# One more order of the pieces of a transformer layer: 392 places, the fillers and who starts the restacking DMAs

## The reference

```python
for i in range(NL):                                       # NL = 6
    xn = _adaln(x, noise_emb, n1_w[i], n1_b[i])
    q, k, v = jnp.split(xn @ qkv_w[i].T, 3, axis=-1)
    q, k = _rope(q.reshape(B, L, H, HD)), _rope(k.reshape(B, L, H, HD))
    ...
    x = x + _attn(q, k, v, src_mask).reshape(B, L, D) @ so_w[i].T
    xn = _adaln(x, noise_emb, n2_w[i], n2_b[i])
    q = _rope((xn @ cq_w[i].T).reshape(B, L, H, HD))
    k = _rope((context @ ck_w[i].T).reshape(B, LC, H, HD))
    ...
    x = x + _attn(q, k, v, ctx_mask).reshape(B, L, D) @ co_w[i].T
    xn = _adaln(x, noise_emb, n3_w[i], n3_b[i])
    x = x + (jax.nn.gelu(xn @ f1_w[i].T + f1_b[i], approximate=False) @ f2_w[i].T + f2_b[i])
```

## Time and profile before

| | us |
|---|---|
| runs of the kernel before | 3232.94, 3234.14, 3237.18 (median 3234.14) |
| profiled execution | 3232.67 |
| its span, first to last instruction | 3230.8 |
| PE busy in the span | 2923.1 (90%) |
| DVE busy | 2161.5 (67%) |
| ACT busy | 1896.3 (59%) |
| POOL busy | 820.1 (25%) |
| DVE, L816, the maxima of self attention | 961.1 |
| ACT, L686, the exponentials | 943.0 |
| PE, L533, values of self attention | 509.2 |
| PE, L360, fillers | 262.7 |

### The profile page before, as it was taken

The page is one execution under the profiler, slowest core; times in us unless marked ns, Lnnn a source line. Parts: engine busy times, 40 slices in busy tenths (PEclk is TensorE's granted clock), DMA queues, the critical chain, the costliest instruction groups (busy, mean ns, idle before and its releaser), DMA issues.

```text
span 3230.8 us, 44892 instructions
## 1 busy us (share of the span) xinstructions
PE 2923.1 (90%) x15691; PEld 1031.2 (32%) x15691; DVE 2161.5 (67%) x3813; ACT 1896.3 (59%) x2677; POOL 820.1 (25%) x1327
## 2 busy tenths in 40 slices
PE   7998999979999999999999857999999998999978
PEld 2474344322322223232232222232322223232226
DVE  4316887658496786958668377769596776858634
ACT  5533444437667585766758534858577585766742
POOL 0003555532212222232213102212222222231211
PEclk9999999989999999999999877999999999999989
DMA  1101000001111111111101001111111111111130
GB/s 46 59 1 27 1 1 1 12 22 41 39 28 39 36 40 37 45 33 37 42 25 49 28 8 42 31 31 49 40 35 34 44 31 37 50 34 32 40 128 7
DMA packets 125506, 110.10 MB, mean 34 GB/s; under 512 B 49978, under 2 KB 116068, under 8 KB 125284
## 3 DMA queue, kind: packets, MB, share of 16 engines
q1 hardware_dynamic: 108004, 91.51, 9.5%
q10 hardware_dynamic: 17280, 15.74, 1.6%
HBM read 41.96 MB, written 0.52 MB: 13 GB/s over the span
## 4 chain that ended last, share of the span: by engine, by line
PE 66%; DVE 14%; SPq 8%; ACT 5%; issue 3%; DMA 3%; POOL 1%; ACTq 0%; DVEq 0%; POOLq 0%
PE ps L533 11%; SPq L437 8%; PE ps L471 6%; DVE arena L816 5%; PE ps L504 4%; PE ps L360 4%; PE ps L602 3%; PE ps L645 3%; DMA arena<-arena 3%; PE ps L661 3%; PE ps L1531 3%; PE ps L479 3%; PE ps L1519 2%; PE ps L574 2%; PE ps L585 2%
## 5 line engine op out<-in xcount | busy, mean ns | idle before, releaser
L686 ACT ACTIVATE arena<-ps 128x1024 f32<-128x1024 f32 x960 | 943.0, 1022 | 184.6 <-PE ps L504 180.0
L816 DVE TENSOR_REDUCE arena<-ps 128x1 f32<-128x512 f32 x1536 | 961.1, 684 | 100.9 <-PE ps L471 92.3
L533 PE MATMUL ps<-arena 128*32 128x512 f32 x3840 | 509.2, 609 | 1.2
L471 PE MATMUL ps<-arena 49*128 49x512 bf16 x1536 | 382.2, 389 | 83.9 <-DMA arena<-arena 37.0
L504 PE MATMUL ps<-arena 52*128 52x512 bf16 x1920 | 348.8, 387 | 34.0 <-ACT arena L686 22.0
L818 DVE TENSOR_REDUCE arena<-ps 128x3 f32<-128x462 f32 (+1 forms) x576 | 305.3, 580 | 110.9 <-PE ps L479 106.3
L913 POOL TENSOR_TENSOR arena<-arena,zeros 128x16 bf16<-128x16 f32 x192 | 42.4, 221 | 1192.6 <-DVE arena L816 769.0
L360 PE MATMUL ps<-consts 128*128 128x512 f32 x508 | 262.7, 624 | 24.4 <-DVE arena L2123 23.7
L471 PEld LDWEIGHTS ps<-arena 49*128 49x128 bf16 x1536 | 101.9, 93 | 498.3 <-DVE arena L816 419.9
L923 POOL TENSOR_TENSOR arena<-arena 128x512 f32<-128x512 f32 x96 | 122.8, 1279 | 323.2 <-ACT arena L716 323.2
L1596 ACT ACTIVATE arena<-ps 128x1024 f32<-128x1024 f32 x96 | 98.3, 1023 | 156.1 <-DVE ps L1681 152.8
(11 more groups left out here) (385 smaller groups left out, 4272.3 us busy)
## 6 DMA issues: line engine op xcount, KB each, us to landing
arena<-arena SPq DMA_DIRECT2D x624, 64.0 KB
arena<-arena ACTq DMA_DIRECT2D x240, 64.0 KB
arena<-we_dram SPq DMA_DIRECT2D x24, 578.5 KB, 7.7
w<-weights_dram SPq DMA_DIRECT2D x26, 320.0 KB, 3.1
w<-weights_dram SPq DMA_DIRECT2D x13, 512.0 KB, 4.1
arena<-arena SPq DMA_DIRECT2D x384, 6.0 KB
arena<-arena SPq DMA_DIRECT2D x288, 19.2 KB
w<-weights_dram SPq DMA_DIRECT2D x39, 128.0 KB, 2.2
```

The source lines that it names most:

```text
L471: pe.matmul(s_bank(slot + r), qst[b][rows, idx, P * qt:P * (qt + 1)], kst[b][rows, idx, :], start=True, stop=True).then_inc(s_full, 1)
L533: mm = pe.matmul(bank(7)[32 * j:32 * j + 32, :], v, prob[:, slot, j, :], start=(g % 2 == 0 and kt == 0), stop=(a == 0 and g % 2 == 1 and k ...
L686: act.activation(prob[:, chunk_no(b, a, g, kt) % NPROB, 2 * p:2 * p + 2, :], e_bank(slot).rearrange("p (j n) -> p j n", j=2), ACT.Exp, sca ...
L816: op = ve.tensor_reduce(nmax[:, g % 2, r, n:n + 1], s_bank(slot + r), AX.X, ALU.max, negate=True)
```

## The change

It gives another list of places for the same 392 pieces, another set of fillers and another set of slots that ScalarE begins (8 and not 10 in a layer). The code that runs a piece is the same. Of the table, whose rows tell little by themselves, three lines stand here:

```diff
-    ('inv', 0): [[134, 160], [297, 304]],
+    ('inv', 0): [[117, 153], [293, 303]],
-    ('f2',): [327, 428],
-    ('gain',): [-77, 95, 227],
+    ('f2',): [330, 430],
+    ('gain',): [-78, 86, 304],
...
-        ACT_STACKS = (("st", 0, 0, 2), ("st", 0, 1, 0), ("st", 0, 2, 5), ("st", 1, 0, 0), ("st", 1, 0, 4),
-                      ("st", 1, 1, 1), ("st", 1, 1, 2), ("st", 1, 1, 5), ("st", 1, 2, 1), ("st", 1, 2, 3))
-        FILL = {('center', 0, 0): 1, ('center', 0, 2): 1, ('out', 0, 1): 1, ('out', 1, 1): 3, ('proj', 1, 2):
-                1, ('score', 0, 0, 0, 2): 1, ('score', 0, 0, 0, 5): 1, ('score', 0, 0, 0, 6): 1, ('score', 0,
-                0, 0, 7): 1, ('score', 0, 0, 1, 0): 1, ('score', 0, 0, 1, 4): 1, ('score', 1, 1, 0, 0): 2,
-                ('var', 0, 2): 1}
+        ACT_STACKS = (("st", 0, 0, 0), ("st", 0, 1, 4), ("st", 1, 0, 0), ("st", 1, 0, 1), ("st", 1, 0, 4),
+                      ("st", 1, 1, 5), ("st", 1, 2, 0), ("st", 1, 2, 1))
+        FILL = {('center', 0, 2): 1, ('out', 0, 1): 1, ('out', 1, 1): 3, ('score', 0, 0, 0, 1): 1, ('score',
+                0, 0, 0, 2): 1, ('score', 0, 0, 0, 3): 1, ('score', 0, 0, 0, 4): 1, ('score', 0, 0, 0, 7): 1,
+                ('score', 0, 0, 1, 0): 1, ('score', 0, 0, 1, 4): 1, ('score', 1, 0, 0, 0): 1, ('score', 1, 0,
+                2, 1): 1, ('score', 1, 1, 0, 0): 2, ('var', 0, 2): 1}
```

More of the change, by code:

```diff
@@ L131 @@
-    ('st', 1): [[63, 78, 83, 80, 64, 81], [91, 73, 70, 88, 87, 85], [308, 311, 317, 309, 310, 312]],
-    ('ktail',): 185,
-    ('vals',): [4, 119, -1],
-    ('f1',): [[320, 323], [424, 426]],
-    ('f2',): [327, 428],
-    ('gain',): [-77, 95, 227],
-    ('biasf',): 167,
-    ('load',): {'cout': 560, 'cross': 306, 'ffn': 584, 'n0': 46, 'n1': 284, 'n2': 392, 'self': 174, 'sout':
-        341},
+    ('score', 0, 0): [[0, 1, 2, 3, 4, 5, 7, 8], [9, 11, 15, 18, 19, 22, 24, 29], [33, 35, 37, 41, 43, 45, 48,
+        50], [56, 69, 72, 77, 82, 87, 89, 93]],
@@ new lines @@
+    ('score', 0, 1): [[228, 230, 233], [236, 239, 245], [250, 255, 259], [263, 265, 273]],
+    ('score', 1, 0): [[98, 101, 104, 108, 111, 115, 118, 122], [125, 128, 130, 134, 136, 139, 144, 146], [154,
+        155, 159, 161, 166, 168, 172, 174], [176, 183, 190, 197, 203, 205, 208, 211]],
+    ('score', 1, 1): [[317, 318, 320], [321, 323, 325], [333, 336, 338], [341, 343, 349]],
+    ('msplit', 0, 0): [12, 39, 57, 103],
+    ('msplit', 0, 1): [240, 251, 260, 275],
+    ('msplit', 1, 0): [124, 151, 184, 217],
@@ new lines @@
+    ('pv', 1, 0): [[160, 178, 179, 194], [201, 209, 213, 215], [231, 237, 241, 248], [252, 257, 264, 269]],
+    ('pv', 1, 1): [[346], [363], [372], [373]],
+    ('tail',): [[274, 290], [344, 370]],
+    ('pvt',): [[[282, 288], [298, 299]], [[364, 367], [374, 381]]],
+    ('evac', 0): [[92, 148], [289, 300]],
+    ('evac', 1): [[216, 270], [368, 382]],
+    ('sel', 0): [[97, 152], [292, 301]],
+    ('sel', 1): [[227, 272], [377, 384]],
+    ('inv', 0): [[117, 153], [293, 303]],
+    ('inv', 1): [[232, 276], [378, 385]],
@@ new lines @@
+    ('out',): [[164, 307], [285, 388]],
+    ('center',): [[-55, 170, 312], [44, 291, 402]],
+    ('var',): [[-50, 175, 313], [49, 295, 408]],
+    ('apply',): [[-44, 180, 315], [55, 296, 419]],
+    ('proj',): [[-39, -37, 185, 83], [58, 61, 302]],
+    ('hi',): [[-36, -31, 189, 113], [62, 66, 305]],
+    ('st', 0): [[-12, -16, -17, -26, -3, -30], [-21, -2, -13, -1, -6, -9], [200, 221, 224, 199, 219, 222], [119,
+        191, 186, 162, 169, 193]],
+    ('st', 1): [[65, 76, 94, 64, 75, 63], [67, 79, 84, 81, 80, 90], [309, 311, 316, 308, 310, 306]],
@@ L140 @@
+    ('ktail',): 218,
+    ('vals',): [6, 150, -5],
+    ('f1',): [[319, 322], [426, 428]],
+    ('f2',): [330, 430],
+    ('gain',): [-78, 86, 304],
+    ('biasf',): 243,
+    ('load',): {'cout': 539, 'cross': 335, 'ffn': 533, 'n0': -45, 'n1': 246, 'n2': 405, 'self': 196, 'sout':
+        324},
 }
```

60 lines of the change are left out of this document (17 added, 43 removed).

## The result

The changed kernel takes 3,215.55 us (median of six runs, 3,212.27 to 3,225.77), the kernel before on the same chip 3,233.92 us (3,225.64 to 3,238.47). The ratio is 0.995, 95% interval 0.9934 to 0.9966: about 18 us faster, where 17 were forecast. The span of the profiled execution is 3,210.2 us, before 3,230.8.

A forecast was written before the change was run, and what follows sets the result against it. PE was taken as the fullest engine, with DVE, PE or a chain of waits setting the pace by stretch. Terms summed to -1.4 us a layer, times 12 -16.8, from 3,232.7 to 3,215.9, plus 1.5: 3,217 us; range 3,202 to 3,243.

The forecast's parts named there:

- Join: Between layers: `vals 2` no longer stands between the first two scores, so DVE's gap goes; -0.3 us a layer (-0.6 to 0).
- Restacking for batch 1: Before batch 1's first score: SyncE begins 16 DMAs, not 14, mostly covered by DVE's shuffle; +0.3 us (0 to +1.4).
- Cross query of batch 0: Its restacking: SyncE's 12 DMAs, before 10, cost +1.3 us, cancelled by earlier rope work; 0 (-0.5 to +1.3).
- PE's work: Up to batch 1's norm: `gain 2` and a PV piece leave the full stretch, a filler enters; -0.4 us (-1.0 to +0.5).
- The denominators ahead of the variance: Batch 1's cross norm: earlier inverse keeps POOL's multiplication off DVE's TENSOR_SCALAR; -0.8 us a layer (-0.9 to +0.3).
- FFN of batch 0: `f2 0` starts about 1.2 us later, more scores precede the norm's matmuls, DVE gaps pay; -0.2 us (-0.9 to +1.2).
- Last restacking: End of the layer: 20 DMAs on SyncE as before; 0.
- the full engine: Rival, no change: PE waits at the next place for what it gains; 3,228 to 3,240, middle 3,234 us; chance 0.18.
- The clock: Rival, slower: with two fillers gone nearby, one more clock fall in each layer adds 30 us; 3,247 us; chance 0.11.
- SyncE's queue: Rival, slower: both additional slots paid whole, PE's work gives nothing, layer 1.4 us longer; 3,251 us; chance 0.11.
- three marks set for "wrong": Batch 1's first score waits over 1 us; clock 0.50 in most layers; norm behind `f2 0` later than 169.3 us.
- marks for "right": TENSOR_SCALAR 0.49 us; second-score gap under 0.2; 16 DMAs about 11.2; DVE idle under 0.4; layers near 188.8 us.

The follow-up runs named there:

- e5: The changed kernel with `vals 2` behind the first score of a layer again, its fillers unchanged: 3,237.59 us, ratio 1.0009 to the kernel before.
- e12: e9 with slot (1,1,2) of batch 1's restacking begun by ScalarE, so SyncE has 14 DMAs there, not 16: 3,202.97 us, ratio 0.99.
- e7: The changed kernel with `gain 2` back at its earlier place, in the stretch that PE fills: 3,226.91 us, ratio 0.9964.
- e11: e9 without the one filler that the change put ahead of a score of batch 1: 3,206.77 us, ratio 0.9894.
- e1: The changed kernel with `inv 0,1,0` behind the variance of batch 1's cross norm again: 3,217.86 us, ratio 0.995.
- e2: The kernel before with only `inv 0,1,0` moved ahead of the variance of batch 1's cross norm: 3,232.32 us, ratio 1.0002.
- e9: The changed kernel with the multiplication of `inv 0,1,1` done by VectorE behind its rope, not by POOL: 3,203.58 us, ratio 0.9895.
- e8: The changed kernel with the pieces around `f2 0` (places 319 to 342) in the order of the kernel before: 3,226.48 us, ratio 0.997.
- e6: The changed kernel with two fillers back, ahead of batch 1's cross query projection and batch 0's next norm: 3,225.19 us, ratio 0.9969.
- e3: The changed kernel with POOL's multiplication of `inv 0,1,1` waiting for the rope's sum L872 on DVE: 3,221.58 us, ratio 0.9946.
- e10: The kernel before, old order, with both multiplications `inv 0,1,*` on VectorE and not POOL: 3,231.52 us, ratio 0.9976.

## Why the prediction was right, step by step

The forecast was right: 3,217 for 3,215.55 us, faster. That it was right to 1.5 us is in good part luck: four terms were off in size or mechanism, and their errors went both ways (batch 1's restacking and the denominators came out some 0.8 and 0.6 us a layer worse than forecast, PE's work and the FFN 0.8 and 0.4 better). The forecast was -1.4 us a layer; measured are -1.5 over ten layers, -1.2 by the medians of clean layers and -0.8 in the pair of the table, whose rows the parts below follow:

- *Join*: -0.3 forecast, -0.47 measured at the second score. That it counts at all is shown by e5.
- *Restacking for batch 1*: +0.3 forecast. Measured, the join's gain and 0.68 more are gone at that score, +1.1. SyncE starts 0.7 us sooner in the layer (0.3 forecast) and ends 0.7 later, with 1.46 more of issuing; the shuffle was the cover named, but DVE still idles 0.64. It lies near the upper end of the range given (+1.4), and it is the largest miss in size. The sentence that SyncE is full for its 9.80 us was true, and the conclusion from it was half of the matter: the transfers need as long, within a microsecond, and 1.2 us less issuing gave 0 to 0.3 in e12. The Trainium skill (DMA: Bandwidth & Descriptors, "Issuing engines are not separate DMA queues") says that issuing from several engines saves only the sequencer's time, which is usually small beside the transfer. e12 agrees with the first half, which I had set aside; the second does not hold here, with 11.26 us of issuing beside some 11 us of transfers.
- *Cross query of batch 0* and *PE's work*: 0 and -0.4 forecast, from batch 1's first score to the norm -1.2 measured. `gain 2` is 0.6 of it (e7). The PV piece that went ahead of batch 1's first score can give up to 1.06, which no run tests. The filler that I had set against it costs nothing (e11), since DVE sets the pace where it stands: that was the error. (The change has one more filler there than the prediction counts, ahead of batch 1's very first score; PE still waits 0.70 us behind it.)
- *The denominators ahead of the variance*: -0.8 forecast. L853 became fast as said, -0.86 up to the norm's application, and 0.69 went back at L872, 3 us further on. This is the step that failed: the path. I had taken the chain to the restacking to run through the norm, and it ran through POOL's second multiplication, behind which L872 ends by 0.55 us in every layer. e1 and e2 measure the net as 0.15 to 0.17 us, e9 shows what lay behind it. The Trainium skill (SBUF — State Buffer, "Who interferes with whom") says that a VectorE instruction with two SBUF inputs and a GpSimd instruction that reads SBUF exclude each other, and that the later one waits for the whole of the earlier. The trace agrees: DVE's sum started 0.06 us behind POOL's multiplication, took 1.75 - 0.69 = 1.06 us more than alone, and ended 0.55 us behind it. I had quoted it and not looked for the next meeting, although L872 took 1.07 us and not 0.69 already in the kernel before.
- *FFN of batch 0*: -0.2 forecast, -0.60 measured. Undoing its order (e8) gives back 0.33 up to the norm, counted from the layer's start. The filler that the change took out ahead of that norm is the other part: with it back (e6) the way from `f2 0` to the norm is 7.54 us and not 6.67. The two are more than the 0.60 together; I have not separated them further.
- *Last restacking*: 0 forecast. The layer of the table loses 0.5 us there. But from the end of SyncE's last issue to the first score on PE it takes 1.72 to 2.39 us in the layers of before and 1.91 to 2.40 after, in no order, so this looks like scatter.

Of the rivals, the full engine would have given 3,234: PE's place as the bound held, but in the waits beside it there was something to gain. The clock's place was named rightly; its count went from four to five in the ten layers. SyncE's queue was half right, as said. Of the three marks set for "wrong" two did not come: the first score of batch 1 waits 0.70 us and not over 1, and the norm behind `f2 0` is applied at 167.55 us (168.0 by the prediction's start of a layer), not behind 169.3, but for the layers with low clock. The third, a clock of 0.50 somewhere in most layers, did come as it stands: in eight of all twelve. It was a poor mark, since the kernel before has it in seven. Of the marks for "right" the idle DVE (0.64 for 0.4) failed.

A sum and a count of the prediction are wrong and moved nothing else: all low ends together are -3.9 us a layer and not -3.4, so 3,187 and not 3,193; and the 64 reductions are those of one batch, of 128 a layer, 106 of which lie in the two stretches named.

## What to carry to other kernels

Where an instruction is slow because it meets one of another engine, look for the next pair that will meet, before pricing the move, and find out which of the two sets the end. Giving both pieces of work to one engine, one behind the other, ended the collision and gained (e9, -12 us); a wait ended it too and cost as much elsewhere (e3), and in the old order the same exchange of engines cost nearly as much as it gave (e10). A move between two full stretches is priced by which engine sets the pace where the piece arrives and where it leaves: 1.06 us of filler were free beside DVE's maxima (e11), and 0.61 us of `gain 2` were paid in full where PE was the bound (e7). Fewer DMAs on one issuing engine help only until the transfers themselves are the longer of the two.
